# Edge keys' rows and source score rows of a two-layer graph kernel: stored in DRAM and read back by all partitions instead of turned on TensorE

## The reference, cut to what matters

```python
# x: (1250, 768); src, dst: (21250,) edges sorted by dst, self loops included. Two blocks, each
# x = x + GAT(LN(x)) + mixer(LN(x)), then a routed FFN. Block 0's GAT has two layers of 4 heads:
h = (x @ W).reshape(-1, 4, 192)
as_ = sum(h * a_src, -1); ad_ = sum(h * a_dst, -1)             # source and target scores, (1250, 4)
e = leaky_relu(as_[src] + ad_[dst], 0.2)
e = exp(e - segment_max(e, dst)[dst]); alpha = e / segment_sum(e, dst)[dst]
out = segment_sum(h[src] * alpha, dst)
# block 0's mixer: linear attention, 8 heads of 96, 256 random features, then a projection
# block 0's FFN: one pooled router picks 2 of 4 experts; block 1: one-head GAT layers, elu mixer, 8 gated experts
```

## Time and profile before

| | us |
|---|---|
| median of 3 runs (2638.74 to 2639.62) | 2639.05 |
| profiled execution | 2642.76 |
| its span, first to last instruction | 2641.0 |
| PE busy | 2567.0 (97%) |
| DVE busy | 1586.7 (60%) |
| ACT busy | 779.6 (30%) |
| POOL busy | 347.4 (13%) |

### The profile page before, as it was taken

One profiled execution on the slowest core, in us unless ns is written; L12 is line 12 of the kernel. 1 busy time (PEld: TensorE's weight loads), 2 busy tenths in 40 slices (PEclk: granted clock), 3 DMA queues, 4 the chain that ended last, 5 costly groups with the idle time before them and its releaser, 6 DMA issues.

```text
span 2641.0 us, 26830 instructions
## 1 busy us (share of the span) xinstructions
PE 2567.0 (97%) x10673; PEld 1821.8 (69%) x10673; DVE 1586.7 (60%) x2708; ACT 779.6 (30%) x1314; POOL 347.4 (13%) x197
## 2 busy tenths in 40 slices
PE   7999999999999997999999999999999999999999
PEld 4667667558965987777777775465755786556676
DVE  4456471789948996997788998254432461341322
ACT  1043342016732873222222221430002431342000
POOL 0888888000000000000000000000000000000000
PEclk9999999999999998999999999999999999999999
DMA  9232313543020406000120002200350100213201
GB/s 255 23 46 14 50 2 49 142 124 104 20 60 0 106 11 214 1 0 1 72 100 2 24 24 85 99 1 0 97 182 18 36 0 1 59 35 131 86 24 59
DMA packets 138070, 155.70 MB, mean 59 GB/s; under 512 B 96524, under 2 KB 108390, under 8 KB 136418
## 3 DMA queue, kind: packets, MB, share of 16 engines
q1 hardware_dynamic: 67225, 153.56, 18.8%
q0 software_dynamic: 70720, 0.43, 2.8%
HBM read 117.75 MB, written 35.83 MB: 58 GB/s over the span
## 4 chain that ended last, share of the span: by engine, by line
PE 51%; DVE 7%; ACT 2%; issue 1%; DMA 0%; SPq 0%; DVEq 0%; ACTq 0%
PE psum L523 50%; DVE arena L1878 2%; DVE arena L1880 1%; DVE arena L1879 1%; PE psum L534 0%; DVE arena L1871 0%; ACT arena L1140 0%; ACT arena L1145 0%; ACT arena L1031 0%; DVE arena L1536 0%; DVE arena L1944 0%; DVE arena L1378 0%; DVE arena L1877 0%; DVE arena L1870 0%; DVE arena L1903 0%
## 5 line engine op out<-in xcount | busy, mean ns | idle before, releaser
L523 PE MATMUL psum<-arena 128*125 128x384 f32 (+12 forms) x9762 | 2459.8, 413 | 39.0 <-DMA arena<-in_ffn_w 7.1
L523 PEld LDWEIGHTS psum<-arena 128*125 128x125 f32 (+3 forms) x9762 | 1721.0, 188 | 751.5 <-issue 136.4
L2293 POOL DMA_INDIRECT count_matrix<-arena x170 | 342.8, 2016 | 122.8 <-DVE arena L1475 60.9
L1878 DVE RECIPROCAL arena<-arena 128x500 f32<-128x500 f32 x60 | 196.7, 3278 | 2.1
L1628 DVE CUSTOM_DVE_ANT_0 arena<-arena 125x1250 bf16<-125x1250 bf16 (+1 forms) x100 | 139.2, 1457 | 12.9 <-ACT arena L1173 12.3
L2303 POOL MEMSET arena<- 125x60 f32 x1 | 0.2, 207 | 1047.0 <-PE psum L523 1047.0
L1712 DVE TENSOR_TENSOR arena<-arena 125x1250 f32<-125x1250 f32 x80 | 116.3, 1453 | 18.5 <-ACT arena L1122 18.3
L1119 ACT ACTIVATE arena<-arena 125x1250 f32<-125x1250 f32 x80 | 106.9, 1336 | 54.5 <-PE psum L523 54.2
L1715 DVE SCALAR_TENSOR_TENSOR arena<-arena 125x1250 f32<-125x1250 f32 x80 | 116.9, 1461 | 2.8
L1031 ACT ACTIVATE arena<-psum 128x250 f32<-128x250 f32 (+1 forms) x102 | 40.6, 495 | 231.9 <-PE psum L534 231.5
L1265 ACT ACTIVATE arena<-psum,arena 128x250 f32<-128x250 f32 x120 | 49.3, 465 | 198.3 <-PE psum L523 198.3
(11 more groups left out here) (223 smaller groups left out, 1463.9 us busy)
## 6 DMA issues: line engine op xcount, KB each, us to landing
arena<-in_ffn_w SPq DMA_DIRECT2D x3, 4608.0 KB, 15.4
residual<-arena SPq DMA_DIRECT2D x30, 336.0 KB
arena<-residual SPq DMA_DIRECT2D x30, 336.0 KB
arena<-target_rows SPq DMA_DIRECT2D x12, 610.4 KB
arena<-in_gat_w SPq DMA_DIRECT2D x3, 2304.0 KB, 9.4
arena<-residual SPq DMA_DIRECT2D x10, 672.0 KB
residual<-arena SPq DMA_DIRECT2D x10, 672.0 KB
count_matrix<-arena SPq DMA_DIRECT2D x2, 3125.0 KB, 27.0
```

The lines of the kernel that those rows point to most:

```text
L523: return pe.matmul(o, lhsT, rhs, start=start, stop=stop, skip_group_check=share)
L1878: now(dve.reciprocal(t_, t_))
L2293: pool.indirect_dma_start(counts[k], bass.IndirectOffsetOnAxis(ap=IDX_I[0:T, c:c + 1].bitcast(U32), axis=0), COUNT_I[0:T, c:c + 1], None, ...
```

## The change

Key groups: the edges are loaded turned (column c of the old layout is now 125 consecutive edges, partition c of `KEYT`), DVE makes the keys there, two PE transposes give `KEY`, SP stores `KEYT` to `key_dram`, and each group's row of up to 500 keys is read back by 125 partitions into one of two buffers (`key_rows_load`), SP waiting for the group two before to be used. PE's 170 transposes are gone. The order of SP's first DMAs, the places of the groups and the batches (2, ten times 4, 1) are other than before. Source scores: in layer 0 one transpose of all 40 columns, copied, stored, and per head read back by all partitions (`source_row`); in layer 1 the scores lie as rows already (`SCT`) and are stored from there. The 80 transposes (`asrow`) and their copies are gone. The last head of layer 1 runs in the order of the others, and ACT's first normalisation waits for all its banks.

```diff
-KEYS_BESIDE = [0] * 6 + [2, 3] + [1] * 12
+KEYS_BESIDE = [0] * 4 + [1, 1] + [1, 1, 1, 0, 1, 1, 0, 1, 1, 0, 1, 1, 0, 1]
 KEYS_BESIDE_QK = [1] * 6
-KEYS_AFTER_HEAD = [4] * 5 + [0] * 3
+KEYS_AFTER_HEAD = [4] * 6 + [1] + [0]
+KEY_BATCHES = [2] + [4] * 10 + [1]
...
-        seq += {0: [("turned_s", 0)], 1: [("asrow", 0), ("asrow", 1)], 8: [("asrow", 2)]}.get(t, [])
+        seq += {0: [("turned_s", 0)]}.get(t, [])
     for t in range(NT):
         seq.append(("h", (t, 1)))
-        seq += {2: [("asrow", 3)], 4: [("rows", 0)], 5: [("step", 0)], 8: [("step", 1)]}.get(t, [])
+        seq += {4: [("rows", 0)], 5: [("step", 0)], 8: [("step", 1)]}.get(t, [])
...
+    V.append(("keyt",))
...
+        KEY_ROWS = [mem(edges_at, KEYG * T), in_d(KEYG * T)]
...
-            keys = list(range(NKEY))
-
-            def key_rows():
-                i = keys.pop(0)
-                pe.wait_ge(keys_made, 1)
-                b = fill("V", ("key", i))
-                for j in range(min(KEYG, EC - i * KEYG)):
-                    c = i * KEYG + j
-                    last = pe.transpose(b[0:T, j * T:(j + 1) * T], KEY[0:T, c:c + 1].to_broadcast([T, T]),
-                                        IDENT[0:T, 0:T])
-                last.then_inc(v_filled, 1)
+            pe.wait_ge(keyt_made, 1)
+            b = fill("V", ("keyt",))
+            pe.transpose(b[0:T, 0:128], KEYT[:, 0, :], IDENT)
+            pe.transpose(b[0:T, 128:EC], KEYT[0:EC - 128, 1, :], IDENT[0:EC - 128, 0:EC - 128]).then_inc(v_filled, 1)
...
-                for _ in range(KEYS_AFTER_HEAD[h]):
-                    key_rows()
...
+            b = fill("A", ("ast",))
+            pe.transpose(b[0:H0 * NT, 0:T], ASC[0:T].rearrange("p a b -> p (a b)"), IDENT[0:T, 0:T]).then_inc(a_filled, 1)
...
-                if t == 4:
-                    pe.wait_ge(v_drained, V_AT[("mask", NT - 1, 2)] + 1)
-                for h in ASROW_AFTER.get(t, ()):
-                    column_rows(("asrow", 0, h), ASC[:, h, :])
...
-                    by_pairs = 4 if (layer, h) == (1, H0 - 1) else 0
-                    for j in range(NT - by_pairs):
+                    for j in range(NT):
...
-                    for b in range(5 if by_pairs else 0):
-                        for j in range(NT - by_pairs, NT):
-                            n = (layer * H0 + h) * NT + j
-                            if b == 0:
-                                pe.wait_ge(et_made, n + 1)
-                            for i in range(2):
-                                last = mm(banks[b][0:T, i * (C0 + 1):(i + 1) * (C0 + 1)],
-                                          ET4[n % 4][0:T, (2 * b + i) * T:(2 * b + i + 1) * T], hn(layer, j, h),
-                                          False, j == NT - 1, share=True)
-                        last.then_inc(v_filled, 1)
...
-                if stage == 1 and g == 3:
+                if stage == 1 and g == 0:
...
+                if (layer, i) == (1, 0):
+                    act.wait_ge(as_saved, 32)
...
+            dve.wait_ge(edges_loaded, 64)
+            for i, p in parts:
+                step(dve.tensor_copy(SRCTF[p, i, :], SRCT[p, i, :]))
+                step(dve.tensor_copy(KEYT[p, i, :], DSTT[p, i, :]))
+            after(own[0])
+            step(dve.scalar_tensor_tensor(KEYT[:, 0, :], SRCTF[:, 0, :], float(N), KEYT[:, 0, :], ALU.mult, ALU.add))
+            p = parts[1][1]
+            now(dve.scalar_tensor_tensor(KEYT[p, 1, :], SRCTF[p, 1, :], float(N), KEYT[p, 1, :], ALU.mult, ALU.add))
+            dve.engine_nop().then_inc(keyt_made, 1)
...
+                if i == 1:
+                    dve.wait_ge(v_filled, V_AT[("keyt",)] + 1)
+                    dve.tensor_copy(KEY[0:T], bank(("keyt",))[0:T, 0:EC]).then_inc(v_drained, 1)
+                    dve.wait_ge(consts_made, NCONST)
+                    now(dve.tensor_copy(TRASH[0:T], TRASHI[0:T]))
+                    dve.wait_ge(v_drained, 1)
...
-                dve.wait_ge(v_filled, V_AT[("key", i)] + 1)
-                b = bank(("key", i))
+                dve.wait_ge(rows_loaded[i % 2], 16 * (i // 2 + 1))
                 for j in range(min(KEYG, EC - i * KEYG)):
                     c = i * KEYG + j
-                    row = b[0:T, j * T:(j + 1) * T]
+                    row = KEY_ROWS[i % 2][0:T, j * T:(j + 1) * T]
...
-                if i % 5 == 4 or i == NKEY - 1:
+                if i + 1 in ends:
...
+                if t == 0 and layer < 2:
+                    dve.wait_ge(asrow_loaded[h % 2], 16 * (2 * layer + h // 2 + 1))
...
             x = w["x"]
-            for i in range(5):
+            for o, name in ((SRCT, "src"), (DSTT, "dst")):
+                flat = w[name].rearrange("t c -> (t c)").rearrange("(c p) -> c p", p=T)
+                load(o[:, 0, :], flat[0:128], edges_loaded)
+                load(o[0:EC - 128, 1, :], flat[128:EC], edges_loaded)
+
+            def x_load(i):
                 tile_load(Y[0:T, 2 * i:2 * i + 2, :], x[250 * i:250 * (i + 1), :].rearrange("(a p) d -> p a d", a=2), x_loaded[i])
-                if i == 1:
-                    load(W[:, :, 0:HALF], w["mix0_wv"][:, :, 0:HALF], wv_loaded[0])
-                if i == 2:
-                    row_load(0, "mix0_bv", bv_loaded)
-            load(SRCI[0:T], w["src"], edges_loaded)
-            load(DSTI[0:T], w["dst"], edges_loaded)
-            load(W[:, :, HALF:], w["mix0_wv"][:, :, HALF:], wv_loaded[1])
-            sp.wait_ge(zeros_made, 1)
-            for k in range(2):
+
+            def zeros_store(k):
                 load(counts[k].rearrange("(p c n) o -> p c (n o)", p=128, c=NT // 2),
                      ZERO.bitcast(U16).unsqueeze(1).to_broadcast([128, NT // 2, 2 * N]), zeros_written)
+
+            def key_rows_load(first, last):
+
+                for i in range(first, last):
+                    if i >= 2:
+                        sp.wait_ge(rows_used, i - 1)
+                    n = min(KEYG, EC - i * KEYG)
+                    row = key_dram[i * KEYG:i * KEYG + n, :].rearrange("c p -> (c p)").rearrange("(o n) -> o n", o=1)
+                    load(KEY_ROWS[i % 2][0:T, 0:n * T], row.to_broadcast([T, n * T]), rows_loaded[i % 2])
+
+            x_load(0)
+            load(W[:, :, 0:HALF], w["mix0_wv"][:, :, 0:HALF], wv_loaded[0])
+            x_load(1)
+            row_load(0, "mix0_bv", bv_loaded)
+            sp.wait_ge(keyt_made, 1)
+            load(key_dram[0:128], KEYT[:, 0, :], keyt_saved)
+            load(key_dram[128:EC], KEYT[0:EC - 128, 1, :], keyt_saved)
+            sp.wait_ge(zeros_made, 1)
+            x_load(2)
+            zeros_store(0)
+            sp.wait_ge(keyt_saved, 32)
+            key_rows_load(0, 2)
+            x_load(3)
+            zeros_store(1)
+            x_load(4)
+            load(W[:, :, HALF:], w["mix0_wv"][:, :, HALF:], wv_loaded[1])
...
+            key_rows_load(2, 14)
             vf(("v", NT - 1, 1))
-            pieces_load(WS8[:, :, 2 * H0:], w["gat1_w"], gw_loaded[1])
+            pieces_load(WS8[:, :, 2 * H0:], w["gat1_w"], gw_loaded[1], lambda k: key_rows_load(14 + k, 15 + k))
             sp.wait_ge(v_drained, V_AT[("v", NT - 1, 1)] + 1)
             row_load(0, "gat0_ad", grow_loaded[0])
             for blk in range(2, 5):
                 vf(("q", blk - 2, 2))
                 block_load(blk)
+                if blk > 2:
+                    key_rows_load(4 * blk + 8, 4 * blk + 12)
+            key_rows_load(28, 32)
             sp.wait_ge(wa_kept, 1)
             pieces_load(WS8[:, :, 2 * H0:], w["gat0_w"], gw_loaded[0])
             vf(("q", 3, 2))
             block_load(5)
+            key_rows_load(32, NKEY)
...
+            def source_row(layer, h):
+                if h > 1:
+                    sp.wait_ge(max_done, layer * H0 + h - 1)
+                row = as_dram[layer, h * NT:(h + 1) * NT, :].rearrange("t q -> (t q)").rearrange("(o n) -> o n", o=1)
+                load(ASROWS[layer][h % 2][0:T], row.to_broadcast([T, N]), asrow_loaded[h % 2])
+
+            def beside_projection(t):
                 for j in COUNTS_BESIDE.get(t, ()):
                     count_load(j)
-
-            residual(0, x, SLOT_M, res[XMID0], later_counts, begun=True)
+                if t == 0:
+                    sp.wait_ge(a_drained, A_AT[("ast",)] + 1)
+                    load(as_dram[0], AST[0:H0 * NT], as_saved)
+                if t == 6:
+                    sp.wait_ge(as_saved, 16)
+                    sp.wait_ge(v_drained, V_AT[("mask", NT - 1, 2)] + 1)
+                    source_row(0, 0)
+                    source_row(0, 1)
+                if t == 9:
+                    source_row(0, 2)
+
+            residual(0, x, SLOT_M, res[XMID0], beside_projection, begun=True)
+            source_row(0, 3)
...
+            sp.wait_ge(a_drained, A_AT[("s", 2)] + 1)
+            load(as_dram[1].rearrange("(a t) q -> a (t q)", a=H0), SCT[0:H0], as_saved)
+            sp.wait_ge(as_saved, 32)
+            for h in range(H0):
+                source_row(1, h)
```

(52 more changed lines are left out.)

20 lines of the change are left out of this document (8 added, 12 removed).

## The result

The changed kernel takes 2662.57 us (median of 5 runs, 2656.05 to 2667.32) against 2639.62 for the kernel before beside it (5 runs, 2638.74 to 2642.29): a ratio of 1.0085, 95% interval 1.007 to 1.0099, some 23 us slower by the medians. The forecast was 2635.5, its range 2625 to 2649. The profiled execution is 2662.57, 19.8 us over the one of before.

The account below looks back on a forecast made before the run. PE is busy 97%, but before the first mask POOL's scatter was expected to decide. Keys +5.3 +0.5, layer 0 -2.9, layer 1 -4.9, last head -1.5, together -3.5, gave 2635.5 us, range 2625 to 2649.

Parts of the forecast that it names:

- the sixth product: Mixer's sixth value product: needs value bank 1, free at 51.7 after pair 4's late landing, so PE stands 7.2 us.
- Rival C: Key comparisons reading both operands from SBUF hold up POOL once per column: 46 us, 2681; chance 0.02.
- Layer 1: Source rows in layer 1: 40 transposes spared, row stored and loaded before DVE's first maximum; -4.9 us, bounds 2 and 4.9.
- The last head: Layer 1's last head in plain order: matmuls end 8 us sooner, DVE's drains limit the gain to 1.5 us.
- 41 key rows, 0.12 us each, 5 us: Key row reads during the scatter delay POOL's indirect DMAs by 5 us in all; bounds 0 and 20.
- rival B: Key rows take engines from the indirect DMAs, POOL stands 0.4 us for each: 16.4 instead of 5, 2647; chance 0.22.
- 0.21 us per load: Cost of each of 41 key row reads to POOL's scatter from which rival B was said to decide (8.5 / 41).
- PE would be at the masks by 455: Before the first mask: PE, spared 23.4 us of key work, arrives by 455 and finds the counts not there.
- some 15 us: PE's standing time before the first mask, waiting for the scatter; 0.5 us added for a longer time at lower clock.
- the 3.3 us of the earlier trace: 16 key transposes hold PE 3.3 us after a head; five heads were counted as 13.5 us of PE's saving.
- the new start: Later x loads and new batches: POOL stands 6 us, ninth column at 83.7, scatter ends at 467.4 against 467.12, nothing won.
- Layer 0: Source rows in layer 0: 4.9 us of transposes spared, PE waits 2 for DVE's later first maximum; -2.9, bounds 0 and 4.9.

Follow-up runs that it names:

- without the reads: Changed kernel reading only key rows 0 and 1, all later groups compared with these, edges set apart beforehand instead of merged; 2639.7 us, ratio 1.0001.
- the spare reads: Kernel before plus 40 unused reads of 500 numbers to each of 125 partitions, at the changed kernel's key-read places; 2672.76 us, ratio 1.0116.
- the experiment with a quarter of the turns: Kernel before with one key transpose per group instead of four (43 instead of 170), edges set apart beforehand; 2639.94 us, ratio 1.0003.
- Source rows alone: Kernel before with only the source score rows stored and read back, keys and last head as before; 2630.15 us, ratio 0.9966.
- the last head alone: Kernel before with only layer 1's last head in the order of the other heads; 2639.35 us, ratio 0.9994.

## Why the prediction was wrong

**What held.** Pair 3's statistics were forecast at 36.3 and began at 35.52; pair 4's statistics were forecast at 47.0 and began at 47.51; the first drain for the sixth product at 51.7, which began at 51.99; POOL's first scatter at 59.4, it was 61.51. Rival C (a lock between DVE and POOL, 46 us) is refuted: DVE compared from SBUF, and POOL's operation stayed at 1986 ns (median); of the lock in the Trainium skill ("SBUF — State Buffer", section "SBUF: two separate sides") no run here shows a sign. Layer 1 was forecast at -4.9: the stretch from the turns of layer 0's output to layer 1's first head product fell from 110.5 to 104.9 us (751.67 to 862.16, and 779.58 to 884.46). The last head was forecast at -1.5 and fell from 54.06 to 51.6 (its first product to the router's; 966.24 to 1020.30, and 988.52 to 1040.12): its matmuls take 33.65 us instead of 43.0, then PE is 5.28 us idle, and its turns take 4.64 us for 2.72, at a granted clock of 0.58, most of it at the lower of the two levels. Alone it measured the same -2.5 in its trace.

**The step that failed** is the term "41 key rows, 0.12 us each, 5 us" of the scatter's side. Measured, it is 23.2 us (mask of the changed kernel less mask without the reads), 0.57 us for each read, or up to 2 us more in all, since that division is good to 2 us only; the spare reads in the kernel before cost 0.76 each. The waits for a DMA grew by 37.8 (51.2 less 13.4 without reads), of which 14.9 came back, since POOL then waited less for its own issue (38.1 for 46.7) and for the index (59.7 for 66.0). That is beyond my upper bound of 20 for the sum and beyond rival B, which had the mechanism and took 0.4 each. The row that I took, 15.4 us over some fifty loads, was of loads of other shapes, nearly all of them to 128 partitions; I had worked out from the earlier trace rows that a key row keeps 5 of 16 engines for 2.2 us and used it for the landing of x, but not for the price to others. The nearest bound was in my own numbers: an indirect DMA that comes while its engines are taken can wait for as long as the row takes, 2.2 us, and more when a weight load follows (4.64 us at 171.02).

Two numbers of rival B were wrong as well. For the landing of an indirect DMA it had 5 us against two periods of 2.29; the trace of before has 3.7 (median). So there is some 0.9 us to spare (4.58 - 3.7, an estimate) before POOL waits, which fits that most weight loads left no wait and that a row which holds engines for 2.2 us leaves one. The longest landing is 8.0 us in the changed kernel and 6.1 before. And "0.21 us per load" is not where B decides: to pass 2644.3 the reads must cost the 5 us of the sum and 8.8 more, 0.34 each.

The rule of the Trainium skill ("DMA: Bandwidth & Descriptors", section "Why a DMA increments its semaphore by 16 and not by 1") that 125 rows go to 5 engines agrees with what 128 partitions for 125 do here: waits of 31.3 for 53.6 with the spare reads, 29.4 for 51.2 in the changed kernel. The same page of the Trainium skill (section "Queues, rings and completion order") has an engine take turns between queues by packets of some descriptors; with 2000-byte rows such a turn is long, with 500-byte rows short, which would fit 53.6 against 22.9. No run here shows an engine's turns, and the shorter time that a read of a quarter of the bytes takes as a whole would fit as well; which of the two it is stays open.

**The second error** changed no number of the forecast, but its cover. "PE would be at the masks by 455": it came at 487. The 455 is the old 477.8 less 23.4; it leaves out the 8.7 us by which the same section has the sixth product begin later (51.7 for 43.0), and it does not go with the "some 15 us" that PE should stand before a mask at 483. With them it is about 461 (435.88 + 39.77 + 8.7 - 23.4). Of the rest, 14.2 us are the reads' (487.0 less 472.8 without them). Of the 23.4 us, 13.5 were of the turns behind heads, and I read the 3.3 us of the earlier trace rows as PE's. They were mostly the time until DVE had drained the head's products, which PE waits for either way: the experiment with a quarter of the turns removed 13.4 us of busy time for 5.7 of arrival. Then DVE itself waits, in program order, for rows that SP may only load into a free one of two buffers, and what PE needs stands behind (timeline of DVE in the changed kernel):

```profile
145.08 0.35 DVE L1431 SCALAR_TENSOR_TENSOR arena<-arena 125x125 f32<-125x125 f32 x1 [3.45 <-DMA arena<-key_rows]
...
249.25 0.35 DVE L1431 SCALAR_TENSOR_TENSOR arena<-arena 125x125 f32<-125x125 f32 x1 [3.35 <-issue]
```

Each of these waits is followed by a stall of PE, 7.84 us at 152.36 and 5.79 at 258.91. Without the reads the stalls there are 4.93 and 1.70.

**Third, a term of the right kind and too small:** the new start. I had POOL idle 6 us before the ninth column and the end unmoved at 467.4; without reads it idled 5.4 and ended at 471.3, 3.9 later. Nearly all of that stands at the ninth column, forecast at 83.7: it came at 87.38 without reads, at 85.32 in the changed kernel. There POOL's gap was 1.1 us, not the 6 that I named as a sign, since it had already waited for DMAs between its first eight columns. PE stood 4.7 us at the sixth product for a forecast of 7.2: x came as forecast, but PE was done with the fifth at 47.3, not at 44.5, and the sixth took 5.65 us, not 3.9.

**Layer 0** was -2.9 with bounds 0 and -4.9. Source rows alone: from first mask to first head product 136.0 us against 140.1 with the last head alone, whose first mask also came without a stall: -4.1, within the bounds, since the row landed 7.2 us after its issue and DVE's first maximum was 65.3 us behind the mask (66.4 before), not 2.1 later. In the changed kernel it took 9.7 us to land and only 0.9 was gained, then 1.5 lost in the heads behind a stall of 3.08 us. Why this row landed later there was not settled.

The sum, put right: scatter, reads +23.2, start +4.0; layer 0 -0.9 and +1.5, layer 1 -5.6, last head -2.5: +19.8 before rounding, the difference of the two profiled executions.

## What to carry to other kernels

Before work is taken off the busiest engine, follow the other chain to the same meeting point: here PE and the scatter reached the first mask within 2 us of each other, so 13 us of PE's work was worth nothing, while of POOL's longer waits 60 to 80% arrived at the mask (23.2 of 37.8 us, 30.4 of 38.2). A broadcast read is not free because its own landing is covered: price it by what it does to the small DMAs beside it. Here fewer bytes and more engines each took off about half of its price, so give such a read a partition count that uses all engines, even where a few partitions are thrown away. And try the parts of a joint change apart: two of these three gain 11 us, the third loses 33.

## What the runs showed of the hardware

40 reads of 250 KB each, spread over an idle-looking DMA system (share 0.35, 57 GB/s), slowed 170 indirect DMAs of 125 two-byte elements: the waits for them grew by 38 us, the time by 1.16%. 128 partitions for 125, with more bytes, left 16 us and 0.51%; a quarter of the bytes left 7.5 us and 0.49%; whether the source is one address or 125 made no difference to the waits (53.1 and 53.6). An indirect accumulating DMA of this size cost POOL 1.99 us (median) in all fourteen kernels here. PE's clock stood at its lower level (granted clock 0.50) behind 17.8, 8.8 and even 4.6 us of standing: the mask that took 1.35 us without such a stall took 2.43 behind each.
